# A fused Mamba and graph-attention block: 48 places instead of 64 in the attention's loop rounds, and another order on two engines in the steps that hold scans and tokens

## What is computed

```python
x = x + conv(ln_c(x))     # two Mamba blocks: s = _ln(_mamba(...)), silu(s @ W_mid), s = _ln(_mamba(...)), silu(s + r)
t = to_tokens(x)          # 16 * 1024 = 16384 tokens of 128 values
t = t + ffn(ln_t(t))
# in the Mamba block, for each channel:
h = dA_t * h + dBx_t      # dA = exp(dt * A), dt = softplus(...)
# in ffn: attention over 524288 random edges (src, dst in 0..32767) and one loop for each node
e = leaky_relu(a_src[src] + a_dst[dst]); e_max = segment_max(e, dst)
ee = exp(e - e_max[dst]); denom = segment_sum(ee, dst)
agg = segment_sum(h[src] * ee / denom, dst)      # 4 heads x 4 experts
# scores = mean over heads of layernorm(agg); the best two of 4 experts mix hh @ W2 + b2, hh = gelu(x @ W1 + b1)
```

## Time and profile before

| | |
|---|---|
| median of 3 runs | 4289.58 us (4286.68 to 4291.24) |
| the profiled execution, its time | 4290.37 us |
| its span | 4288.4 us |
| PE busy | 2896.4 us, 68% |
| DVE busy | 3026.0 us, 71% |
| ACT busy | 1552.8 us, 36% |
| POOL busy | 1345.1 us, 31% |
| mean granted clock of PE | 0.819 |

### The profile page before, as it was taken

One profiled execution on the slowest core, in us unless ns is written; L12 is line 12 of the kernel. 1 busy time (PEld: TensorE's weight loads), 2 busy tenths in 40 slices (PEclk: granted clock), 3 DMA queues, 4 the chain that ended last, 5 costly groups with the idle time before them and its releaser, 6 DMA issues. The chain is left out here.

```text
span 4288.4 us, 30277 instructions
## 1 busy us (share of the span) xinstructions
PE 2896.4 (68%) x9220; PEld 1468.0 (34%) x9220; DVE 3026.0 (71%) x4723; ACT 1552.8 (36%) x2238; POOL 1345.1 (31%) x1414
## 2 busy tenths in 40 slices
PE   6988798999999899897648155445545544453019
PEld 2433343444444344343335022223322322232019
DVE  8899879887888697978664556546645654664565
ACT  2332145444445444444454033223223322322117
POOL 0000000000000000001111677777777777777600
PEclk9998899999999999998768567767767776776559
DMA  5113123445454455466546321122112111111237
GB/s 177 69 69 115 57 89 95 145 147 171 145 176 146 155 158 191 155 183 236 191 148 221 28 44 37 37 45 47 37 37 54 37 37 45 27 18 18 23 140 285
DMA packets 341083, 454.19 MB, mean 106 GB/s; under 512 B 82749, under 2 KB 256712, under 8 KB 332090
## 3 DMA queue, kind: packets, MB, share of 16 engines
q1 hardware_dynamic: 289290, 389.20, 28.2%
q0 software_dynamic: 51632, 63.07, 7.8%
HBM read 340.70 MB, written 111.42 MB: 105 GB/s over the span
## 5 line engine op out<-in xcount | busy, mean ns | idle before, releaser
L1487 POOL DMA_INDIRECT got<-scratch_tab,src_at x1280 | 1223.6, 956 | 390.0 <-issue 378.4
L691 PE MATMUL in_ps<-tokens,w_in 128*128 128x512 f32 x2048 | 938.4, 610 | 20.3 <-ACT zst L898 15.6
L1441 PE MATMUL hid_ps<-tokens,w 128*128 128x512 f32 x512 | 314.1, 746 | 834.9 <-ACT hid L1669 812.2
L618 POOL MEMSET tokens<- 1x128 int32 x1 | 0.2, 194 | 1899.9 <-DVE tokens L1073 1899.9
L691 PEld LDWEIGHTS in_ps<-tokens,w_in 128*128 128x128 f32 x2048 | 394.4, 197 | 501.9 <-issue 501.9
L708 PE MATMUL out_ps<-w_out,act 128*128 128x512 f32 x1024 | 476.9, 609 | 4.6 <-DMA w_out<-in_m_WoutT 4.5
L1072 DVE TENSOR_TENSOR tokens<-tokens 128x1024 f32<-128x1024 f32 x380 | 464.4, 1222 | 9.7 <-ACT tokens L856 8.7
L1073 DVE TENSOR_TENSOR tokens<-tokens 128x1024 f32<-128x1024 f32 x380 | 464.0, 1221 | 0.0
L1441 PEld LDWEIGHTS hid_ps<-tokens,w 128*128 128x128 f32 x512 | 107.7, 234 | 928.7 <-ACT hid L1669 822.1
L1594 DVE TENSOR_TENSOR hold<-by_value,is_loop 128x256 f32<-128x256 f32 x20 | 8.5, 425 | 581.7 <-ACT by_value L1680 581.7
L1680 ACT ACTIVATE by_value<-got 128x1536 f32<-128x1536 f32 x20 | 80.5, 4027 | 743.6 <-DMA got<-scratch_tab,src_at 743.6
(11 more groups left out here) (270 smaller groups left out, 4053.6 us busy)
## 6 DMA issues: line engine op xcount, KB each, us to landing
w_out<-in_m_WoutT SPq DMA_DIRECT2D x256, 512.0 KB, 4.7
w_in<-in_m_WinT SPq DMA_DIRECT2D x128, 512.0 KB, 4.0
scratch_y<-ys SPq DMA_DIRECT2D x25, 1024.0 KB, 4.0
got<-scratch_tab,src_at POOLq DMA_INDIRECT x1280
tokens<-scratch_xt SPq DMA_DIRECT2D x8, 2048.0 KB, 9.4
scratch_sz<-zst SPq DMA_DIRECT2D x64, 256.0 KB, 5.4
gz<-scratch_sz SPq DMA_DIRECT2D x64, 256.0 KB, 5.1
tokens<-scratch_y SPq DMA_DIRECT2D x16, 1024.0 KB, 8.6
```

The lines of the kernel that those rows point to most:

```text
L691: last = t_.matmul(in_ps[:, z, :], w_in[:, n % WIN, k, :], xT[:, s % 2, k, :], start=(k == 0), stop=(k == KC - 1))
L1441: last = t.matmul(hid_ps[:, f], w1[:, e, f * P:(f + 1) * P], tokens[:, g * QW:(g + 1) * QW], start=True, stop=True)
L1487: g.indirect_dma_start(got[:, y, t, :], None, tab_d[:, :], bass.IndirectOffsetOnAxis(ap=src_at[:, y, t:t + 1], axis=0))\
```

## The change

Two parts. In the attention, rounds of the loop have `FD` = 48 places: 48 gathers, and the merge that feeds such a round counts only the first 48 of its 64 merged keys and marks the others as edges. The tiles and the loads of keys keep 64 places. The three copies that carry the running state from one round to the next (`logit`, `add`, `hold1`, from place n) move from the start of `compute` to its end, so POOL clears these three tiles once at the start. The trips are now (longest list + 224 - 1152) / 96, rounded down, at least 1; the division by 96 is a shift by 5, a product with 21846 and a shift by 16.

In the steps t = 67 to 73 ScalarE gets another order. On VectorE, `tokens_second` moves into `scan`, ahead of the wait for the decays.

```diff
@@ -48,2 +48,5 @@
 LOG_2FR = 7
+FD = 48
+LOG_GROUP = 5
+THIRD = 21846
 ROW = H16 + 2 * HEADS
@@ -1010,2 +1013,19 @@
                     root((t, 0))
+                    if t > TOK_AT and j <= NJ:
+                        decay(j - 1)
+                        tokens_copy(t - TOK_AT - 1, 0)
+                        root((t, 1))
+                        tokens_root(t - TOK_AT)
+                        if j < NJ:
+                            softplus(j)
+                        tokens_normal(t - TOK_AT)
+                        if j < NJ:
+                            logarithm(j)
+                        if t in outs_at and outs_at[t] % 4 == 0:
+                            put_out(outs_at[t])
+                        tokens_copy(t - TOK_AT - 1, 1)
+                        if outs_at.get(t, 0) % 4:
+                            put_out(outs_at[t])
+                        root((t, 2))
+                        continue
                     if begun:
@@ -1116,3 +1136,3 @@
 
-                def scan(j):
+                def scan(j, token):
 
@@ -1127,2 +1147,3 @@
                         kb(v.tensor_tensor(h0, dtu[x], bc[:, 0, :], ALU.mult))
+                        tokens_second(token)
                         v.wait_ge(s_dec, j + 1)
@@ -1148,2 +1169,4 @@
                         v.tensor_tensor(u, h0, gz[:, x, :], ALU.mult).then_inc(s_y, 1)
+                    else:
+                        tokens_second(token)
 
@@ -1268,4 +1291,3 @@
                     tokens_first(t - TOK_AT)
-                    scan(t - SCAN_AT - 1)
-                    tokens_second(t - TOK_AT)
+                    scan(t - SCAN_AT - 1, t - TOK_AT)
                     norms((t, 2))
@@ -1308,7 +1330,8 @@
                         ck(v.tensor_reduce(len_max, len_f.rearrange("x o p -> x (o p)"), AX.X, ALU.max))
-                        ck(v.tensor_scalar(slots_i, len_max, float(P + 1 + 2 * FR - 1), None, ALU.add))
-                        ck(v.tensor_scalar(slots_i, slots_i, LOG_2FR, None, ALU.logical_shift_right))
-                        ck(v.tensor_copy(len_max, slots_i))
-                        ck(v.tensor_scalar(rounds_i[:], len_max, float(PAIRS + 1), float(PAIRS), ALU.max,
-                                           ALU.subtract))
+                        ck(v.tensor_scalar(len_max, len_max, float(2 * FD - 1 + P + 1 - 2 * FR * PAIRS), float(2 * FD),
+                                           ALU.add, ALU.max))
+                        ck(v.tensor_copy(slots_i, len_max))
+                        ck(v.tensor_scalar(slots_i, slots_i, LOG_GROUP, None, ALU.logical_shift_right))
+                        ck(v.tensor_scalar(slots_i, slots_i, THIRD, None, ALU.mult))
+                        ck(v.tensor_scalar(rounds_i[:], slots_i, 16, None, ALU.logical_shift_right))
                         v.sem_inc(s_rnd, 1)
@@ -1410,3 +1433,3 @@
             def rounds(eng):
-                return eng.value_load(rounds_i[0:1, 0:1], min_val=1, max_val=((NE + P + 2 * FR) >> LOG_2FR) - PAIRS)
+                return eng.value_load(rounds_i[0:1, 0:1], min_val=1, max_val=(NE + P + 2 * FD) // (2 * FD))
 
@@ -1484,4 +1507,4 @@
 
-                def gather(y):
-                    for t in range(FR):
+                def gather(y, n):
+                    for t in range(n):
                         g.indirect_dma_start(got[:, y, t, :], None, tab_d[:, :],
@@ -1502,2 +1525,5 @@
                 g.memset(peak[:], 0.0)
+                g.memset(logit[:], 0.0)
+                g.memset(add[:], 0.0)
+                g.memset(hold1[:], 0.0)
                 g.memset(one_f[:], 1.0)
@@ -1515,3 +1541,3 @@
                             load_last(1 - y)
-                        gather(y)
+                        gather(y, FR if first else FD)
                         g.wait_ge(s_block, 1)
@@ -1531,3 +1557,3 @@
             def _(v):
-                def merge(ck, r, y, last_on):
+                def merge(ck, r, y, last_on, width):
 
@@ -1550,5 +1576,7 @@
                     ck(v.tensor_scalar(edge_i[:], merged, LOG_M, 1, ALU.logical_shift_right, ALU.bitwise_and))
-                    ck(v.tensor_copy(is_edge[:, y], edge_i[:]))
-                    ck(v.tensor_reduce(n_edge[:], is_edge[:, y], AX.X, ALU.add))
-                    v.tensor_scalar(next_lo[:], next_lo[:], n_edge[:, 0:1], float(FR), ALU.subtract, ALU.add)
+                    if width < FR:
+                        v.memset(is_edge[:, y, width:FR], 1.0)
+                    ck(v.tensor_copy(is_edge[:, y, 0:width], edge_i[:, 0:width]))
+                    ck(v.tensor_reduce(n_edge[:], is_edge[:, y, 0:width], AX.X, ALU.add))
+                    v.tensor_scalar(next_lo[:], next_lo[:], n_edge[:, 0:1], float(width), ALU.subtract, ALU.add)
                     ck(v.tensor_tensor(row_pos[:], row_pos[:], n_edge[:], ALU.add))
@@ -1573,3 +1601,3 @@
 
-                def compute(ck, y):
+                def compute(ck, y, n):
 
@@ -1578,5 +1606,2 @@
                     v.tensor_copy(hold0[:, :, 1:F1], spread(is_edge[:, y], HEADS))
-                    v.tensor_copy(logit[:, :, 0:1], peak[:, :, FR:F1])
-                    v.tensor_copy(add_r[:, :, 0:1], run[:, 0:SUMS, FR:F1])
-                    v.tensor_copy(hold1[:, :, 0:1], a_dst[:, :, FR:F1])
                     ck(v.tensor_tensor_scan(dist_f[:], one_f[:], is_edge[:, y], 0.0, ALU.mult, ALU.add))
@@ -1621,2 +1646,5 @@
                     v.sem_inc(s_packed, 1)
+                    v.tensor_copy(logit[:, :, 0:1], peak[:, :, n:n + 1])
+                    v.tensor_copy(add_r[:, :, 0:1], run[:, 0:SUMS, n:n + 1])
+                    ck(v.tensor_copy(hold1[:, :, 0:1], a_dst[:, :, n:n + 1]))
 
@@ -1627,3 +1655,3 @@
                 ck(v.tensor_copy(next_lo[:], bin_f[:]))
-                merge(ck, 0, 0, 0)
+                merge(ck, 0, 0, 0, FR)
                 v.wait_ge(s_last, 16)
@@ -1638,3 +1666,4 @@
                         if first:
-                            merge(ck, r + y + 1, 1 - y, FIRST_LAST if r + y + 1 == 2 * PAIRS else 0)
+                            turn = r + y + 1 == 2 * PAIRS
+                            merge(ck, r + y + 1, 1 - y, FIRST_LAST if turn else 0, FD if turn else FR)
                             count(ck, b_first[:, (r + y + 1) * FR:(r + y + 2) * FR])
@@ -1642,5 +1671,5 @@
                             v.wait_ge(s_last, 16 * (r + y + 1) - 16 * (2 * PAIRS - 1))
-                            merge(ck, r + y + 1, 1 - y, FR)
+                            merge(ck, r + y + 1, 1 - y, FR, FD)
                             count(ck, b_k[:, 1 - y])
-                        compute(ck, y)
+                        compute(ck, y, FR if first else FD)
                     v.sem_clear(s_mch)
@@ -1675,6 +1704,6 @@
 
-                def pair(i, work=()):
+                def pair(i, work=(), got_before=0):
                     for y in range(2):
                         mine = list(work[y]) if work else []
-                        wait_apart(s, (s_got[y], 16 * FR * i + 16 * FR))
+                        wait_apart(s, (s_got[y], 16 * FR * i + 16 * FR if work else 16 * FD * i + got_before))
                         s.activation(by_value[:], got[:, y].rearrange("p f x -> p x f"), ACT.Copy).then_inc(s_turned, 1)
@@ -1708,3 +1737,3 @@
                 with s.Fori(0, rounds(s)) as i:
-                    pair(i + PAIRS)
+                    pair(i + PAIRS, (), 16 * FR * PAIRS + 16 * FD - 16 * FD * PAIRS)
```

## The result

The changed kernel takes 4230.74 us (median of 4 runs, 4229.39 to 4233.45), the kernel before 4288.88 beside it: ratio 0.9865, 95% interval 0.9848 to 0.9882. It is 58 us faster; the forecast was 4212, its range 4202 to 4237. The profiled execution (4229.39 us) has a span 60.9 us shorter than the one before.

The account below looks back on a forecast made before the run. POOL's gather queue was taken to bound the attention, and a loop of waits across engines steps 67 to 73. 4290.4 - 40.0 - 35.2 - 2.8 = 4212.4, the median 0.8 lower: forecast 4212 us, range 4202 to 4237.

Parts of the forecast that it names:

- rival 1: Steps 67 to 73: weights' loads become the limit, four periods keep their length and three gain; time 4232, chance 0.20.
- The trips and the 40.0 us: Attention: still one loop trip, 1248 gathers instead of 1280, 32 fewer at 1.25 us each, saving 40.0 us.
- 2.8 us in step 66: Step 66: with tokens_second straight behind the root, ACT's idle before normalising image 0 falls from 3.26 to 0.4, 2.8 us earlier.
- Net 5.03 for a period; with seven periods 35.2: Steps 67 to 73: 9.10 us leave the 24.2 us loop and 4.07 enter, saving 35.2 us over seven periods.
- Second copy, table, turn: Steps 67 to 73: links of the new loop from normalising to normalising, whose period was forecast at 19.2 us.
- rival 2: Steps 67 to 73: more than the sum, denser PE work runs nearer full clock, two chunks 3.6 us; time 4203, chance 0.16.
- I take the 8.9 us that layer norms and `put_out` add over all periods as the same on both sides: Steps 67 to 73: these extras add 8.9 us over all periods, equally before and after the change.
- everything after it moves along unchanged: Attention's last round: its copy starts earlier as ACT had idled 55.59 us, and all that follows shifts without change.
- Clears "cost nothing": Attention's start: three added POOL clears, about 2 us, are covered by POOL's 4.99 us wait for the first merge.
- Rival 3: ScalarE: a table swap costs more than its row; 0.3 us by the rows' gaps, 4231 if dear, chance 0.02.
- 4, VectorE in the short rounds: Attention: VectorE bounds the two short rounds, hiding the gain of all 32 gathers; time 4252, chance 0.03.
- 5: one trip: Attention: rival that a longer list makes the loop run twice, 1344 gathers; time 4339, slower, chance 0.02.

Follow-up runs that it names:

- e12: Changed kernel with ScalarE's and VectorE's old orders put back, leaving only the 48 places; 4254.72 us against 4287.13 for the kernel before, ratio 0.9918.
- e6: Changed kernel with ScalarE's old order put back, VectorE's new order kept; image 1's turn to image 8's took 168.5 us.
- e7: Changed kernel with three unread matmuls added on PE ahead of the table's matmul in steps 67 to 71; 4224.47 us against 4287.26 before, ratio 0.9849.
- e3: Changed kernel with the second copy moved straight behind the normalising, ahead of Ln; 4877.31 us against 5007.23 for the kernel before, ratio 0.9735.
- e10: Changed kernel with e3's early second copy and e8's clears on VectorE together; 4215.07 us against 4287.13 for the kernel before, ratio 0.9834.
- e11: e10 with 40 places instead of 48 in the loop's rounds; 4196.85 us against 4287.13 for the kernel before, ratio 0.9783.
- e1: Changed kernel with both engines' old orders put back, only the 48 places kept, on the first group's chip; ratio 0.9829 to the kernel before.
- e5: Changed kernel with VectorE's old order put back (tokens_second behind the scan), ScalarE's new order kept; image 1's turn to image 8's took 169.3 us.
- the first group: Runs e1 to e4 (e4: changed kernel with 40 places, 4864.55 us), on one chip where the kernel before took 5007.23 us.
- e2_order: Changed kernel with the 48 places undone (64 places, no new clears), only the new order kept; 4981.88 us against 5007.23 before, ratio 0.9951.
- e8: Changed kernel with the three added clears moved from POOL to VectorE's setup of the attention; ratio 0.9851 to the kernel before.

## Why the prediction was right, and where not

The time lies in the stated range, 19 us above the forecast and outside the 4204 to 4224 that the sum itself was given. The range reached so far up for rival 1 and for dear table loads, and neither happened; that the result lies in it is luck. The mechanism was right in both parts: the trips, and the loop that no longer runs through decays and scan.

**The trips and the 40.0 us: right.** x1248, one trip, 1.25 us a gather, 40.3 us in the two rounds; the wait read 10.18 for "about 10". e12 shows the term by itself.

**2.8 us in step 66: right.** Turn 0 to turn 1 takes 37.3 us after, 41.3 before, 40.2 in e12 and 38.0 in e6, which has VectorE's half alone. Between after and e12 that is 2.9; all ten profiles with VectorE's new order have 37.3 to 38.3, the four without it 40.0 to 41.3.

**"Net 5.03 for a period; with seven periods 35.2": failed, 24.6.** Three steps inside it were off.
- "Second copy, table, turn" were priced with the table and turn of before (3.06 us from table to chunks). They cost 5.07, as the granted clock falls just when the copy comes; the chunks behind gave 0.39 of that back (4.54 for 4.93). The 3.06 was read from a pair that the low clock just missed; the pairs of images 6 and 7 in the same trace, with 3.61 and 1.95, were not looked at. e7 gives 19.0 for a period once the clock is up. In my rival 2 I had the clock rising with denser work; in the pair it fell, and over the whole stretch from turn 1 to turn 8 it is 0.72 both before and after. What brings it down at just this place no run isolates, beyond e3 and e7, in which less idle time ahead of the pair leaves it up.
- "I take the 8.9 us that layer norms and `put_out` add over all periods as the same on both sides": not so. In step 68 after, `put_out` with its load (2115.71 to 2118.07) stands between the Ln and the second copy, in the loop. e3, with the copy ahead of both, has 18.2 us in that period instead of 23.2, but over this and the next one together 42.9 instead of 44.1, as VectorE is the next wait.
- Step 67 gained nothing since there VectorE was no idle waiter: in the trace of before it waited only 0.83 us for the decays, and the small operations on the trip count and `zst`, 2.6 us (2080.22 to 2082.81), now stand between the scan and the next statistics. One more row of VectorE from that time, after:

```profile
2077.14 3.15 DVE L1135 TENSOR_TENSOR temps<-temps 128x512 f32<-128x512 f32 x1
```

  `step_size` took 3.15 us there, not 0.69. What I had read was step 70, a period from which one cannot multiply by seven. Three later periods gained more than 5.03 (6.4, 6.1 and 6.3), which made up for some of it.

**"everything after it moves along unchanged": not quite.** From the last gather's start to the last block's first operation on VectorE it is 44.4 us instead of 42.1, although the last append starts 0.5 us sooner. All eight profiles with rounds of 48 on chips like this one have it (44.4, once 45.1), e12 with the old order too, so it comes with the 48 places; what the last block waits for there is open.

**Clears "cost nothing": wrong, about 2 us.** I had weighed POOL's queue alone, where the cover of 5.00 us was real. The price came by VectorE, whose operation runs on beside POOL's memset.

**The rivals.** 1, the loads: its time (4232) is the nearest of all to the result, and it is not the cause. From turn 1 to turn 8 PE never waits for `w_out`. Its margin was as thin as it said, though: where the loop is shorter still, PE waits for `w_out` in period 4 to 5, 4.0 us in e3, 3.4 in e10 and 4.6 in e11. In the two periods that gained nothing it waits for ScalarE's copy (PE, after):

```profile
2095.44 3.61 PE L778 MATMUL turn_ps<-zst,tokens 128*128 128x24 f32 x16 [5.62 <-ACT tokens L979]
...
2118.60 3.61 PE L778 MATMUL turn_ps<-zst,tokens 128*128 128x24 f32 x16 [4.43 <-ACT tokens L979]
```

Rival 3, dear table loads: refuted. The load starts at 2157.97, when the operation ahead ends at 2157.96, and Ln starts 0.02 us behind its end. The Trainium skill ("ScalarE: Activation LUTs", What ACT_TABLE_LOAD costs) adds a drain of about 1.38 us to a switch; the rows don't show it, and e7's 19.0 us with three loads in the loop leaves no room for it. 4, VectorE in the short rounds: not with 48 places, and at 40 just reached. 5: one trip; its price is confirmed. 2, more than the sum: no.

**The ledger** of 60.9 us between the two profiled spans (each term rounded): -43.1 in the gathers, -24.6 in the seven periods, -3.9 from turn 0 to turn 1; against it +4.7 ahead of turn 0 (code that is the same in both, and whose time varies by some us from run to run: turn 0 lies between 2030.0 and 2039.5 in the twelve kernels), +4.1 from turn 8 to the first gather (142.9 to 147.0) and +2.1 behind the last gather. Of the 4.1, 2.1 are the merge; 1.7 are period 9-10 (17.8 us instead of 16.1), where two chunks took 5.21 us instead of 3.60 at a granted clock of 0.70 instead of 1.00, both times behind 2.12 us of idle time. e12, with the old order, has 17.8 there too (chunks 5.30, clock 0.69), and e1, the same kernel, and e5 and e7 have 16.1, so it isn't the order's. In the same place, the same code comes out either way.

## What to carry to other kernels

When a wait is taken out of a loop across engines, write the new loop out for every period that differs and price each operation at the state its engine will then be in: a matmul behind an idle stretch gets a range, from the cheapest to the dearest row of its kind (here 1.9 to 3.6 us for the table). What feeds another engine goes first in a queue, ahead of table loads and functions that only fill a slack. Two orders that block one another have to be changed together: either half alone was worth 3 us, both 23. Work moved into an engine's slack can still be paid for by another engine that runs beside it.

## What was unexpected in the hardware

**Late copies on one chip.** On the first group's chip POOL issues a gather every 1.25 us as elsewhere (64 in 79.6 us), yet most rounds start 115 to 123 us apart instead of 83.2. Waits of POOL in e2_order (total us, times, longest), and its last gather of a round and the append behind it:

```profile
POOL scratch_sums L1511 <- ACTq L1717: 736.4, 19, 52.4
```

```profile
3237.22 0.94 POOL L1506 DMA_INDIRECT got<-scratch_tab,src_at  x1 [0.30 <-issue]
3277.15 0.98 POOL L1511 DMA_INDIRECT scratch_sums<-sums,out_at  x1 [38.99 <-ACTq L1717]
```

The append waits for the results of the round before, whose gathered rows ScalarE copied only at 3247.54, 133 us after the last of them was issued at 3114.7. On the other chips the last copy follows 4.0 us behind the last issue. Late landing would explain it, but the DMA view speaks against it: the queue of the gathers has its last packets of that round by 3117, and none between 3117 and 3157. What is slow are the other engines. DVE, PE and ACT of e2_order:

```profile
3187.61 0.23 DVE L1609 TENSOR_TENSOR dist<-dist,moved 128x64 int32<-128x64 int32 x1 [1.29 <-DVE moved L1608]
3206.30 3.56 PE L1460 MATMUL hid_ps<-tokens,w 128*128 128x512 f32 x4 [31.17 <-issue]
3217.58 0.37 PE L1476 MATMUL y_ps<-w,hid 128*128 128x128 f32 x1 [2.54 <-issue]
3247.04 0.60 ACT L1680 ACTIVATE ys<-y_ps 128x512 f32<-128x512 f32 x1 [40.79 <-remote]
3247.54 4.02 ACT L1699 ACTIVATE by_value<-got 128x1536 f32<-128x1536 f32 x1
```

From 3182 on VectorE's small operations, which follow one another within 0.4 us a moment before, are 1.2 to 1.5 us apart, PE idles 2.5 us ahead of single matmuls and waits for nothing that the profile shows, and the copy of the gathered rows stands behind a late copy of the experts' outputs in ScalarE's queue. So POOL waits for engines that were slow; by 3252, some 14 us behind the round's last gather, VectorE has its old pace again. What slowed them is open. It also leaves e1's 88 us open in part. Between e2's and e1's profiles the last two rounds differ by 45 us (205.4 and 160.4), and the first 18, which have 64 places in both, by 52. What differs in that chip was not tried.

**An elementwise operation of VectorE beside work of POOL** took 3.15 us instead of 0.69 (`step_size`) and 2.71 instead of 0.67 (`node_i`). The second went away when POOL's memsets ended before it (e8). The first was not tried by an edit, but the traces compare it: the next `step_size` took 3.18 us in e3, at 2095.14 beside POOL's operation on `w_in` (2095.41 to 2097.76), and 0.69 in the changed kernel, at 2099.98, where POOL's came 2.2 us later. The kernel before has it as well, in a layer norm's operation of 3.66 us instead of 1.22 at 2122.58, with POOL's at 2122.78. In the three slow rows beside that operation VectorE's ends 0.5 to 1.1 us behind POOL's.
